# Layer-norm's x1n computed by GpSimd in place of VectorE in a fused two-layer attention kernel

## The chip, the core and the metric

The kernel runs on one core of a Trainium2 chip. The core has a matrix engine (TensorE, PE in the profile), a vector engine (VectorE, DVE), an activation engine (ScalarE, ACT), a general-purpose engine (GpSimd, POOL) and a queue that issues DMAs (SyncE, SP). Each runs its own instruction stream in order and meets the others only at semaphores. The metric is the time of one execution on the device, in microseconds.

## What is computed

The reference takes x and ctx, each 64 x 128 x 512 in fp32, and applies two layers. The first is an attention over time steps with 1x1 convolutions and a residual; the second a transformer layer, in which x1, the first layer's output, is the residual:

```python
x1 = Wo @ (Ml @ softmax(Mn^T @ Mm)^T) + bo + x          # per item, 128 x 512
q  = layer_norm(x1, ln1_w, ln1_b) @ q_w + q_b           # layer_norm: (x1 - mean) * rsqrt(var + eps) * w + b
k, v = ctx @ k_w + k_b, ctx @ v_w + v_b
h  = softmax(q k^T / sqrt(32)) v @ cproj_w + cproj_b + x1     # 16 heads of 32
out = h + gelu(layer_norm(h) @ fc_w + fc_b) @ proj_w + proj_b
```

The part that matters here is x1n = (x1 - mean) * rstd: one mean and one rstd for each of the 128 rows. The weight and bias of the norm are folded into the projection of q.

## The kernel before

The kernel has two passes. The first, `attention_pass`, takes the 64 items one after another in a software pipeline of slots: slot s works on the first layer of item s (b0), on the end of the first layer of item s-1 (b1), on v, q and k of item s-2 (b2), on the scores and softmax of item s-4 (b4), and on the output of item s-5 (b5). The first seven slots and the last are written out; the ones between are a loop whose body has four slots. Keys are projected for two items at once in slots of even parity, queries in slots of odd parity. The second pass, `mlp_pass`, is untouched by the change.

All matmuls are made in three passes on an upper and a lower half of each operand: ScalarE copies the upper half (`_hi`, rounded), and VectorE or GpSimd subtracts it from the original to get the lower half (`_lo`). The order of the work on each engine is the order of the statements in the function `slot` of that engine.

The path of x1 through a slot boundary: at the end of a slot VectorE adds bias and residual into x1 (L884), takes its statistics (L887, L897, L899), and adds x1b of an older item into hid (L905), which goes out to memory. GpSimd makes rstd by a power (L582), then x1b, the sum of x1 and the projection's bias cproj_bias (L588, a ring of four in the tile that the profile calls stage; it waits for hid of four items before), then ctxT_lo, the lower half of the transposed context (L591), and after it multiplies the four quarters of the probabilities by the reciprocals of their sums (L560). In the next slot TensorE makes the scores (L1006, L1011), projects v (L919 to L921 on bank 2), transposes x1n (L950, four instructions, for which it waits for x1n_set) and then multiplies normed by the convolutions' weights; in a slot of queries the projection of q follows, which waits for xnT_lo. VectorE meanwhile takes maxima of the scores (L783), between the second and third of which stands the normalisation x1n (L804, in place: x1n is x1), then a reciprocal (L779), v plus its bias (L813) and xnT_lo (L759). ScalarE takes xnT_hi from the transposes (L655), then m_hi (L659), exponentials (L633), the bias of q or k (L642, L648) and at_hi (L674), whose lower half at_lo is again VectorE's (L759, then the maxima of L789).

Of the kernel before, what the change touches and what calls it, by code (L numbers as in the profile page):

```python
# [18 lines left out]
ALU = mybir.AluOpType  # L19
# [168 lines left out]
def attention_pass(nc, x, ctx, mask, w, hidden, mlp):  # L188
# [8 lines left out]
    with ExitStack() as stack:  # L197
        def sb(name, shape, dt=F32):
            return stack.enter_context(nc.sbuf_tensor(name, shape, dt))

        def sem(name):
            return stack.enter_context(nc.semaphore(name))
# [38 lines left out]
        x1 = sb("x1", [P, D])  # L241
        x1b = stage[:, 0, :, :]
        x1n = x1
# [24 lines left out]
        x1_mv = sb("x1_mv", [P, 2])  # L268
        x1_ve = sb("x1_ve", [P, 1])
        x1_rstd = sb("x1_rstd", [P, 1])  # L270
# [62 lines left out]
        x1_veps = sem("x1_veps")  # L333
        x1_rstd_ready = sem("x1_rstd_ready")
        x1n_set = sem("x1n_set")
        x1b_set = sem("x1b_set")
        xnT_turned = sem("xnT_turned")
        xnT_hi_set = sem("xnT_hi_set")
# [28 lines left out]
        def weight_hi(i, c):  # L367
            return mlp.first_hi[:, i, c, :] if i < 2 else qc_hi[:, i - 2, c, :]

        def weight_lo(i, c):  # L370
            return mlp.first_lo[:, i, c, :] if i < 2 else qc_lo[:, i - 2, c, :]
# [20 lines left out]
        def slots(eng, slot, ahead=None):  # L392

            for s in range(FIRST, LOOPED):
                if ahead and s in ahead:
                    ahead[s]()
                slot(Batch(0, s, B))
            with eng.Fori(0, TURNS) as turn:
                for s in range(LOOPED, LOOPED + Batch.period):
                    slot(Batch(turn, s, B))  # L400
            for s in range(LOOPED + Batch.period * TURNS, LAST + 1):
                if ahead and s in ahead:
                    ahead[s]()
                slot(Batch(0, s, B))
# [4 lines left out]
        def pair_half(t, e):  # L409

            return t[:, :, e.parity, :]
# [126 lines left out]
        @block.gpsimd  # L538
        def _(pool):
            pool.memset(ident[:], 0.0).then_inc(ident_zero, 1)  # L540
            pool.wait_ge(ident_zero, 1)
            pool.affine_select(out=ident[:], in_=ident[:], compare_op=ALU.not_equal, fill=1.0, base=0,
                               pattern=[[-1, P]], channel_multiplier=1).then_inc(ident_set, 1)
            pool.wait_ge(consts_set, 3)

            def lower_halves(i):

                pool.wait_ge(raw_w_in[i], RAW_W_IN[i])
                for c in range(DC):
                    pool.wait_ge(w_hi_set, 4 * i + c + 1)  # L550
                    pool.tensor_tensor(weight_lo(i, c), raw_w[i][:, c, :], weight_hi(i, c).bitcast(F32),
                                       ALU.subtract).then_inc(w_lo_set[i], 1)

            def slot(s):
                b0, b1, b2, b3, b4, ahead = s, s + -1, s + -2, s + -3, s + -4, s + 1

                def normalise(r):
                    if b4.exists():
                        pool.wait_ge(rsum1_set, b4.nth(4, r + 1))
                        pool.tensor_tensor(probs[:, :, r, :, :], probs[:, :, r, :, :],  # L560
                                           rsum1[:, r, :].unsqueeze(1).unsqueeze(3).to_broadcast([P, 4, 4, 32]),
                                           ALU.mult).then_inc(probs_set, 1)

                if b0.first():
                    lower_halves(K_W)
                for r in range(4):
                    normalise(r)
                if ahead.exists():
                    pool.wait_ge(in_veps, ahead.nth(1, 1))
                    if ahead.has_before(1):  # L570
                        pool.wait_ge(normed_set, (ahead + -1).nth(2, 2))
                    pool.tensor_tensor(in_rstd[:], in_ve[:], neghalf[:, 0:2], ALU.pow).then_inc(in_rstd_ready, 1)
                if ahead.exists():
                    for i in range(2):
                        pool.wait_ge(normed_hi_set, ahead.nth(2, i + 1))
                        pool.tensor_tensor(normed_lo[:, i, :], normed[:, i, :],  # L576
                                           normed_hi[:, i, :].bitcast(F32), ALU.subtract).then_inc(normed_lo_set, 1)
                if b1.exists():
                    pool.wait_ge(x1_veps, b1.nth(1, 1))
                    if b1.has_before(1):  # L580
                        pool.wait_ge(x1n_set, (b1 + -1).nth(1, 1))
                    pool.tensor_tensor(x1_rstd[:], x1_ve[:], neghalf[:, 0:1], ALU.pow).then_inc(x1_rstd_ready, 1)  # L582
                    pool.wait_ge(x1_set, b1.nth(1, 1))
                    if b1.has_before(4):
                        pool.wait_ge(hid_set, (b1 + -4).nth(1, 1))
                    else:
                        pool.wait_ge(vecs_in, 16 * 6)
                    pool.tensor_tensor(x1b[:, b1.quarter, :], x1[:], cproj_bias[:], ALU.add).then_inc(x1b_set, 1)  # L588
                if b0.exists():
                    pool.wait_ge(ctxT_hi_set, b0.nth(1, 1))  # L590
                    pool.tensor_tensor(pair_half(ctxT_lo, b0), ctx_chunks, pair_half(ctxT_hi, b0).bitcast(F32),  # L591
                                       ALU.subtract).then_inc(ctxT_lo_set, 1)
                if b3.first():
                    lower_halves(C_W)

            def first_group():

                mlp.inverse_deviations(pool, Item(0, 0, 1))
                for c in range(STAGE):
                    mlp.lower_half(pool, mlp.first_lo[:, 1, c, :], mlp.first_hi[:, 1, c, :], 1, c, mlp_raw[1])  # L600

            slots(pool, slot, {1: lambda: lower_halves(V_W), LAST: first_group})

        @block.scalar
# [112 lines left out]
        def _(dve):  # L717
# [47 lines left out]
            def slot(s):  # L765
                b0, b1, b2, b3, b4, b5, ahead = s, s + -1, s + -2, s + -3, s + -4, s + -5, s + 1
# [14 lines left out]
                def maxima1(r):  # L781
                    if b4.exists():
                        dve.tensor_reduce(negmax1[:, r, :], by_chunk(S1_BANK[r]), AX_X, ALU.max,  # L783
                                          negate=True).then_inc(max1_set, 1)
# [13 lines left out]
                    dve.wait_ge(s1_done, b4.nth(1, 1))  # L798
                maxima1(0)
                maxima1(1)  # L800
                if b2.exists():
                    dve.wait_ge(x1_rstd_ready, b2.nth(1, 1))
                    dve.wait_ge(x1b_set, b2.nth(1, 1))
                    dve.tensor_scalar(x1n[:], x1[:], x1_mv[:, 0:1], x1_rstd[:, 0:1],  # L804
                                      ALU.subtract, ALU.mult).then_inc(x1n_set, 1)
                maxima1(2)
                maxima1(3)
                sum1_reciprocal(0)
# [98 lines left out]
            def statistics():  # L907
                for t in range(TILES):
                    mlp.statistics(dve, Item(0, 0, 1), t)
                for c in range(STAGE):  # L910
                    mlp.lower_half(dve, mlp.first_lo[:, 0, c, :], mlp.first_hi[:, 0, c, :], 0, c, mlp_raw[0])

            slots(dve, slot, {0: prepare_small, 2: prepare_q, LAST - 2: statistics})

        @block.tensor
# [504 lines left out]
```

## Time and profile before

| | |
|---|---|
| median of 3 runs | 3044.06 us (3041.51 to 3044.44) |
| profiled execution | 3044.57 us, its span 3042.8 us |
| PE busy | 2958.4 us, 97% |
| DVE busy | 1873.4 us, 62% |
| ACT busy | 1471.0 us, 48% |
| POOL busy | 790.0 us, 26% |

The span is the time from the first to the last instruction of the profiled execution; its own time has some 2 us around it. Busy shares are over both passes: the attention pass fills about the first 1630 us, and there VectorE, ScalarE and GpSimd are far busier than the averages say. Instructions that only move semaphores, registers or DMAs are not counted.

### The profile page before, as it was taken

To read this page: it belongs to the slowest core of one execution; us is meant where nothing else is said; L and a number is where in the kernel's file an instruction comes from. 1 tells how busy PE (TensorE), PEld (TensorE's weight loads), DVE (VectorE), ACT (ScalarE), POOL (GpSimd) and SP (SyncE) were. 2 spreads that over 40 slices of the span, in tenths; PEclk is the share of its full clock that TensorE was granted. 3 is DMA by queue.
4 is the path that set the end of the run, shared out by engine and by line. 5 is a ranking of instruction groups with operands and counts; after the bars stand their busy time and mean duration, and the time that the engine had idled before them with its cause. 6 is when DMAs were issued, how large, how long until landed. Compare 5 with 4: busy or idle time off the path is not lost. (4 is left out here: it accounts for less than half of the span.)

```text
span 3042.8 us, 55219 instructions
## 1 busy us (share of the span) xinstructions
PE 2958.4 (97%) x18551; PEld 2474.7 (81%) x18551; DVE 1873.4 (62%) x3705; ACT 1471.0 (48%) x4210; POOL 790.0 (26%) x742
## 2 busy tenths in 40 slices
PE   6999999999999999999977999999999999999999
PEld 5788888888888888888865888888888888888887
DVE  6788888888888888888865433333333333333332
ACT  5777777777777777777753211111111111111111
POOL 4444444444444444444422000000000000000000
PEclk9999999999999999999997999999999999999999
DMA  4355555455555445555444211111111111011110
GB/s 125 101 143 141 145 146 143 134 139 142 140 146 146 139 134 141 141 144 147 137 139 138 70 28 28 38 31 41 41 41 41 28 28 37 32 41 41 41 28 14
DMA packets 336371, 281.80 MB, mean 93 GB/s; under 512 B 149056, under 2 KB 247872, under 8 KB 336320
## 3 DMA queue, kind: packets, MB, share of 16 engines
q1 hardware_dynamic: 336320, 281.15, 33.5%
q8 instruction: 28, 0.46, 0.1%
q14 instruction: 23, 0.19, 0.0%
HBM read 164.68 MB, written 100.66 MB: 87 GB/s over the span
## 5 line engine op out<-in xcount | busy, mean ns | idle before, releaser
L1265 ACT ACTIVATE gl<-pre,fc_bias 128x512 f32<-128x512 f32 x256 | 176.6, 690 | 1119.1 <-PE pre L1350 1119.1
L1304 DVE CAST hT_hi<-gl 128x512 fp32r<-128x512 f32 x256 | 109.2, 427 | 838.3 <-ACT gl L1265 838.3
L633 ACT ACTIVATE rows<-bank,negmax 128x128 f32<-128x128 f32 x1024 | 364.1, 391 | 201.4 <-DVE negmax L783 201.4
L560 POOL TENSOR_TENSOR rows<-rows,rsum 128x512 f32<-128x512 f32 x256 | 266.3, 1041 | 370.7 <-DVE rsum L779 370.7
L1348 PE MATMUL pre<-yT_lo,rest_hi 128*128 128x512 f32 x768 | 298.8, 389 | 0.0
L1349 PE MATMUL pre<-yT_hi,rest_lo 128*128 128x512 f32 x768 | 298.8, 389 | 0.0
L1350 PE MATMUL pre<-yT_hi,rest_hi 128*128 128x512 f32 x768 | 298.8, 389 | 0.0
L1348 PE MATMUL acc<-rest_lo,hT_hi 128*128 128x512 f32 x768 | 298.8, 389 | 0.0
L1349 PE MATMUL acc<-rest_hi,hT_lo 128*128 128x512 f32 x768 | 298.8, 389 | 0.0
L1350 PE MATMUL acc<-rest_hi,hT_hi 128*128 128x512 f32 x768 | 298.8, 389 | 0.0
L576 POOL TENSOR_TENSOR normed_lo<-x_ctx,normed_hi 128x512 fp32r<-128x512 f32 x128 | 163.4, 1297 | 333.1 <-ACT normed_hi L699 333.1
L177 POOL TENSOR_TENSOR rstd<-ve,neghalf 128x4 f32<-128x4 f32 x16 | 16.3, 1018 | 870.1 <-DVE ve L171 870.1
L633 ACT ACTIVATION_READ_ACCUMULATOR rows<-bank,negmax 128x1 f32 x1024 | 235.6, 230 | 0.0
L679 ACT ACTIVATE rows<-bank,negmax 128x512 f32<-128x512 f32 x256 | 175.2, 687 | 65.9 <-DVE negmax L789 65.9
L783 DVE TENSOR_REDUCE negmax<-bank 128x4 f32<-128x512 f32 x256 | 164.0, 682 | 35.0 <-PE bank L1011 34.9
L1306 DVE TENSOR_TENSOR hT_lo<-gl,hT_hi 128x512 fp32r<-128x512 f32 x256 | 177.3, 692 | 8.8
L759 DVE TENSOR_TENSOR at_lo<-bank,at_hi 128x512 fp32r<-128x512 f32 x256 | 169.6, 684 | 11.1 <-ACT at_hi L674 6.0
L789 DVE TENSOR_REDUCE negmax<-bank 128x1 f32<-128x512 f32 x256 | 169.4, 682 | 2.9 <-PE bank L921 2.9
L1350 PEld LDWEIGHTS acc<-rest_hi,hT_hi 128*128 128x128 f32 x768 | 144.2, 188 | 30.1
L1349 PEld LDWEIGHTS pre<-yT_hi,rest_lo 128*128 128x128 f32 x768 | 144.3, 188 | 30.0
L1348 PEld LDWEIGHTS acc<-rest_lo,hT_hi 128*128 128x128 f32 x768 | 144.2, 188 | 29.9
L1348 PEld LDWEIGHTS pre<-yT_lo,rest_hi 128*128 128x128 f32 x768 | 144.1, 188 | 29.9
(160 smaller groups left out, 7857.0 us busy)
## 6 DMA issues: line engine op xcount, KB each, us to landing
p_turn<-rows SPq DMA_DIRECT2D x128, 512.0 KB, 3.0
p_blocks<-p_turn SPq DMA_DIRECT2D x256, 256.0 KB, 5.1
x_ctx<-in_x SPq DMA_DIRECT2D x64, 256.0 KB, 6.1
x_ctx<-in_ctx SPq DMA_DIRECT2D x64, 256.0 KB, 6.5
blocks<-in_ctx SPq DMA_DIRECT2D x256, 64.0 KB, 4.8
small<-in_x SPq DMA_DIRECT2D x64, 256.0 KB, 2.7
hidden<-hid SPq DMA_DIRECT2D x64, 256.0 KB, 2.0
rows<-hidden SPq DMA_DIRECT2D x16, 1024.0 KB, 5.5
```

Of the source, the lines that this page charges most:

```text
L560: pool.tensor_tensor(probs[:, :, r, :, :], probs[:, :, r, :, :], rsum1[:, r, :].unsqueeze(1).unsqueeze(3).to_broadcast([P, 4, 4, 32]), ALU ...
L576: pool.tensor_tensor(normed_lo[:, i, :], normed[:, i, :], normed_hi[:, i, :].bitcast(F32), ALU.subtract).then_inc(normed_lo_set, 1)
L633: act.activation(probs[:, :, r, c, :], by_chunk(S1_BANK[r])[:, c, :].rearrange("p (d b) -> p d b", b=32), ACT.Exp, bias=negmax1[:, r, c:c ...
L679: act.activation(A_cols[:, t, :, :, :], bank[S0_BANK[t]][:].rearrange("p (d c x) -> p d c x", d=4, x=32), ACT.Exp, bias=negmax0[:, t:t + 1 ...
L759: dve.tensor_tensor(out, psum, hi.bitcast(F32), ALU.subtract).then_inc(done, 1)
L783: dve.tensor_reduce(negmax1[:, r, :], by_chunk(S1_BANK[r]), AX_X, ALU.max, negate=True).then_inc(max1_set, 1)
L789: dve.tensor_reduce(negmax0[:, t:t + 1], bank[S0_BANK[t]][:], AX_X, ALU.max, negate=True).then_inc(max0_set, 1)
L1265: act.activation(gl[:, i % 2, :], pre[i % 2][:], ACT.Gelu_apprx_tanh, bias=mlp.fc_bias[:, i:i + 1]).then_inc(gelu_done, 1)
L1306: dve.tensor_tensor(hT_lo[:, i % 2, :], gl[:, i % 2, :], hT_hi[:, i % 2, :].bitcast(F32), ALU.subtract).then_inc(hT_lo_set, 1)
L1348: pe.matmul(out, a_hi, b_lo, start=first, stop=False)
L1349: pe.matmul(out, a_lo, b_hi, start=False, stop=False)
L1350: return pe.matmul(out, a_hi, b_hi, start=False, stop=last)
```

## The change

GpSimd computes x1n behind x1b and ahead of ctxT_lo, in the slot in which x1 is made; VectorE computed it in the slot after. The instruction and its operands are the same. GpSimd waits for its own x1_rstd and x1b first, since x1b reads what x1n overwrites.

```diff
@@ GpSimd
                     pool.tensor_tensor(x1b[:, b1.quarter, :], x1[:], cproj_bias[:], ALU.add).then_inc(x1b_set, 1)
+                    pool.wait_ge(x1_rstd_ready, b1.nth(1, 1))
+                    pool.wait_ge(x1b_set, b1.nth(1, 1))
+                    pool.sem_inc(x1_steps, 1)
+                    pool.tensor_scalar(x1n[:], x1[:], x1_mv[:, 0:1], x1_rstd[:, 0:1],
+                                       ALU.subtract, ALU.mult).then_inc(x1n_set, 1)
@@ VectorE
                 maxima1(1)
-                if b2.exists():
-                    dve.wait_ge(x1_rstd_ready, b2.nth(1, 1))
-                    dve.wait_ge(x1b_set, b2.nth(1, 1))
-                    dve.tensor_scalar(x1n[:], x1[:], x1_mv[:, 0:1], x1_rstd[:, 0:1],
-                                      ALU.subtract, ALU.mult).then_inc(x1n_set, 1)
                 maxima1(2)
```

GpSimd's instructions at the end of the loop's first slot, before the change (stage is the tile that holds x1b, rows the probabilities; in brackets the semaphores waited for):

```order
L582 TENSOR_TENSOR x1_rstd<-x1_ve,neghalf 128x1 [waits x1n_set]
L585 REGISTER_ALU [waits x1_set]
L588 TENSOR_TENSOR stage<-x1,cproj_bias 128x512 [waits hid_set]
L590 REGISTER_ALU
L591 TENSOR_TENSOR ctxT_lo<-small_t,ctxT_hi 128x4x128 [waits ctxT_hi_set]
```

And after it, at the same place:

```order
L583 TENSOR_TENSOR x1_rstd<-x1_ve,neghalf 128x1 [waits x1n_set]
L586 REGISTER_ALU [waits x1_set]
L589 TENSOR_TENSOR stage<-x1,cproj_bias 128x512 [waits hid_set]
L593 TENSOR_SCALAR x1<-x1,x1_mv,x1_rstd 128x512 [waits x1_rstd_ready,x1b_set]
L596 REGISTER_ALU
L597 TENSOR_TENSOR ctxT_lo<-small_t,ctxT_hi 128x4x128 [waits ctxT_hi_set]
```

One instruction has come in between x1b and ctxT_lo, and it waits for x1b's end.

VectorE's instructions at the start of the loop's second slot, before the change (the banks are those of the scores, then of v and of the transposes):

```order
L783 TENSOR_REDUCE negmax1<-bank3 128x4
L804 TENSOR_SCALAR x1<-x1,x1_mv,x1_rstd 128x512 [waits x1b_set,x1_rstd_ready]
L783 TENSOR_REDUCE negmax1<-bank6 128x4
L783 TENSOR_REDUCE negmax1<-bank4 128x4
L778 REGISTER_ALU
L779 RECIPROCAL rsum1<-sum1 128x4 [waits exp1_done]
L813 TENSOR_TENSOR stage<-bank2,v_bias 128x512 [waits v_done]
L759 TENSOR_TENSOR xnT_lo<-bank0,xnT_hi 128x4x128 [waits xnT_hi_set]
```

After the change the same rows stand there without the TENSOR_SCALAR; nothing else has moved.

## Rows read from the trace of the kernel before

**Rows 1.** A stretch's busy us (x): PE, PEld, DVE, ACT, POOL; clock, DMA, GB/s
```profile
1000.00:1500.00 500.00, 495.80 (x4012) 420.05 (x4011) 431.13 (x869) 392.21 (x1232) 216.45 (x207) 1.00 0.51 142
```
**Rows 2.** Who waited for whom: us in total, times, longest us
```profile
PE bank L919 <- DVE xnT_lo L759: 10.6, 31, 1.5
```
**Rows 3.** Timeline, TensorE, four slots' first matmuls (start us, us, engine line op, [idle before])
```profile
1034.64 0.40 PE L1006 MATMUL bank<-mask_less,masked_bf 1*128 1x512 bf16 x4
...
1058.92 0.40 PE L1006 MATMUL bank<-mask_less,masked_bf 1*128 1x512 bf16 x4
...
1082.97 0.40 PE L1006 MATMUL bank<-mask_less,masked_bf 1*128 1x512 bf16 x4
...
1107.07 0.40 PE L1006 MATMUL bank<-mask_less,masked_bf 1*128 1x512 bf16 x4
```
**Rows 4.** Timeline, TensorE, slot of queries from 1034.64
```profile
1041.13 0.36 PE L919 MATMUL bank<-xnT_lo,qc_hi 128*128 128x256 f32 x1 [0.40 <-DVE xnT_lo L759]
```
**Rows 5.** Timeline, VectorE, the same slot
```profile
1037.21 1.32 DVE L804 TENSOR_SCALAR x<-x,x_mv,x_rstd 128x512 f32<-128x512 f32 x1
...
1040.31 0.68 DVE L759 TENSOR_TENSOR xnT_lo<-bank,xnT_hi 128x512 fp32r<-128x512 f32 x1
...
1047.04 0.69 DVE L759 TENSOR_TENSOR at_lo<-bank,at_hi 128x512 fp32r<-128x512 f32 x1 [0.24 <-ACT at_hi L674]
```
**Rows 6.** Timeline, GpSimd, the same slot, then x1b of the next
```profile
1035.70 1.29 POOL L588 TENSOR_TENSOR stage<-x,cproj_bias 128x512 f32<-128x512 f32 x1 [0.88 <-DVE hid L905]
1036.94 1.30 POOL L591 TENSOR_TENSOR ctxT_lo<-small_t,ctxT_hi 128x512 fp32r<-128x512 f32 x1
1039.89 1.04 POOL L560 TENSOR_TENSOR rows<-rows,rsum 128x512 f32<-128x512 f32 x1 [1.65 <-DVE rsum L779]
...
1059.80 1.28 POOL L588 TENSOR_TENSOR stage<-x,cproj_bias 128x512 f32<-128x512 f32 x1 [0.77 <-DVE hid L905]
```
**Rows 7.** Timeline, ScalarE, the slot from 1034.64
```profile
1039.37 0.60 ACT L655 ACTIVATE xnT_hi<-bank 128x512 fp32r<-128x512 f32 x1 [1.14 <-PE bank L950]
...
1044.28 0.84 ACT L648 ACTIVATE qT<-bank,q_bias 128x256 f32<-128x256 f32 x2
```
**Rows 8.** The instructions of line 804: duration ns min/median/max, first and last start
```profile
L804 DVE TENSOR_SCALAR x<-x,x_mv,x_rstd x64: 537/1183/1448, 49.4 to 1566.5; 128x512 f32<-128x512 f32 x64
```
**Rows 9.** A group of instructions on GpSimd: xcount | busy us, mean ns | idle before
```profile
L542 POOL TENSOR_SCALAR_AFFINE_SELECT ident<-ident 128x128 f32<-128x128 f32 x1 | 0.3, 292 | 0.2 <-POOL ident L540 0.2
```
**Rows 10.** Timeline, VectorE and ScalarE, slot of queries from 1082.97
```profile
1085.54 1.12 DVE L804 TENSOR_SCALAR x<-x,x_mv,x_rstd 128x512 f32<-128x512 f32 x1
...
1088.44 0.68 DVE L759 TENSOR_TENSOR xnT_lo<-bank,xnT_hi 128x512 fp32r<-128x512 f32 x1
...
1095.24 0.69 DVE L759 TENSOR_TENSOR at_lo<-bank,at_hi 128x512 fp32r<-128x512 f32 x1
...
1087.70 0.60 ACT L655 ACTIVATE xnT_hi<-bank 128x512 fp32r<-128x512 f32 x1 [1.07 <-PE bank L950]
```
**Rows 11.** Timeline, the loop's entry slot, from its first matmul to the next slot's
```profile
165.78 0.40 PE L1006 MATMUL bank<-mask_less,masked_bf 1*128 1x512 bf16 x4
...
168.50 1.43 DVE L804 TENSOR_SCALAR x<-x,x_mv,x_rstd 128x512 f32<-128x512 f32 x1
...
170.74 0.60 ACT L655 ACTIVATE xnT_hi<-bank 128x512 fp32r<-128x512 f32 x1 [1.36 <-PE bank L950]
...
190.31 0.40 PE L1006 MATMUL bank<-mask_less,masked_bf 1*128 1x512 bf16 x4
```
**Rows 12.** Timeline, slot of keys from 1058.92
```profile
1064.84 0.28 PE L919 MATMUL bank<-ctxT_lo,first_hi 128*128 128x256 f32 x1
...
1071.18 0.69 DVE L759 TENSOR_TENSOR at_lo<-bank,at_hi 128x512 fp32r<-128x512 f32 x1
```
**Rows 13.** Timeline, the slot of the second item's x1n
```profile
71.48 1.29 POOL L588 TENSOR_TENSOR stage<-x,cproj_bias 128x512 f32<-128x512 f32 x1
...
74.34 0.33 PE L950 MATMUL bank<-ident,x 128*128 128x128 f32 x1 [1.14 <-DVE x L804]
```

More of the change, by code:

```diff
@@ L335, in attention_pass @@
         x1n_set = sem("x1n_set")
+        x1_steps = sem("x1_steps")
         x1b_set = sem("x1b_set")
```

## The prediction

> **What bounds the kernel now.** I read the page first, then the engines' busy time in a stretch of the attention pass, then who waited for whom, and at last, slot by slot, the order of time on each engine. In the attention pass TensorE is busy 495.8 us of 500, VectorE 431.1, ScalarE 392.2, GpSimd 216.5 [rows 1]. So a microsecond saved on VectorE is worth nothing unless a matmul waits for it, and a microsecond added to GpSimd costs nothing until a matmul waits for it. The waits say where that is: the first matmul of the queries waited 31 times, 10.6 us in all, for VectorE's xnT_lo [rows 2]. That is two instructions behind the one that moves, and it bounds what the attention pass can plainly gain.
>
> The slots repeat in a pattern of four. I measure everything from a slot's first score matmul (L1006). A slot of keys lasts 1082.97 - 1058.92 = 24.05 us; the slot of queries after it 1107.07 - 1082.97 = 24.10; the other slot of queries, the first after each turn of the loop, 1058.92 - 1034.64 = 24.28 [rows 3]. Call them K, Q and Q'. (The fourth is keys again.)
>
> In Q' the chain reads: GpSimd's x1b ends at 1036.99; ctxT_lo runs to 1038.23; VectorE's x1n starts at 1037.21 and takes 1.32 us, to 1038.53; the transposes follow; ScalarE takes the upper half from 1039.37 to 1039.97; but xnT_lo starts only at 1040.31, since VectorE is late by what it did before; the queries' first matmul starts at 1041.13, and TensorE had been idle 0.40 us for it [rows 4 to 7].
>
> **What x1n costs on VectorE.** Alone it takes 0.54 us, its minimum; its median is 1.18 [rows 8]. It ends 0.28 to 0.30 us behind GpSimd's ctxT_lo in Q' (1038.53 against 1038.23) and in the entry slot too, where it takes 1.43 us. So it sits beside a GpSimd instruction and waits most of its time. The Trainium skill, page "SBUF — State Buffer", section "Who interferes with whom", says that VectorE in a 2-port mode and GpSimd exclude each other by a lock on a shared port pair, and that a tensor_reduce never takes part; by it x1n on GpSimd would meet no holder of that lock, as the maxima are reduces. The trace agrees with the first half (1.18 against 0.54 us).
>
> **The change, part by part.** *Removed*: 64 tensor_scalars from VectorE, one a slot, 1.18 us each, between the second and third maxima. The third and fourth maxima, the reciprocal and the sum with v_bias come earlier. The third maximum has no hurry: ScalarE takes its exponentials after xnT_hi and m_hi. The sum with v_bias now waits for the v projection instead, and xnT_lo for xnT_hi.
>
> *Added*: 64 tensor_scalars on GpSimd behind x1b, with a wait for x1b's end. GpSimd has no such instruction before, so its length is bounded by rows. Below: 0.54 us, VectorE's own undisturbed one. A one-input GpSimd instruction of 128 columns takes 0.29; four times that is 1.17. The multiply whose second operand is a few numbers spread over 512 columns takes 1.04; the two-input sum and difference 1.29 and 1.30 [rows 6, 9]. Above: two operations made in two passes of that, 2.6. I take 1.0, by the multiply, the nearest in reading one full stream. For the wait between x1b's end and the start there is one row: GpSimd waited 0.2 us for its own memset before the affine_select [rows 9]. Back to back, ctxT_lo starts 0.05 us before x1b's end. I take 0.15; bounds 0 and 0.25. So x1n ends 1.15 us behind x1b; bounds 0.55 and 2.85.
>
> The Trainium skill, page "GPSIMD Engine Reference", section 4.1, speaks against the move: elementwise work belongs on VectorE, GpSimd is about twice slower with two inputs, and near line rate with one. Twice the 0.54 us would be an estimate of 1.08 us, and the sum below would be the same by it; no run here shows the instruction yet.
>
> *When it is late.* The transposes are behind the v projection on TensorE. In Q' x1n ended at +3.89 and the upper half began at +4.73 (1039.37); in Q it ended at +3.69 (1085.54 + 1.12) and the upper half began at +4.73 as well (1087.70) [rows 5, 7, 10]. So +3.89 still costs nothing. In the loop's entry slot x1n ended at 169.93, +4.15, and the upper half began at 170.74, +4.96, 0.23 late [rows 11]. Beyond about +3.9 each 0.1 us costs 0.1 us. The new end is +2.35 + 1.15 = +3.50 in Q' and 1061.08 - 1058.92 + 1.15 = +3.31 in K and Q [rows 6]: 0.4 to 0.6 us of cover. x1b cannot start earlier, since it waits for hid.
>
> *Moved*: ctxT_lo starts behind x1n, and ends at 2.16 + 1.15 + 1.25 = +4.56 in K. The first matmul of the keys that reads it starts at 1064.84, +5.92 [rows 12]: 1.36 us of cover. Behind it on GpSimd stands the multiply of the first quarter of probs, at 1039.89, +5.25, in Q'; ctxT_lo ends there at +4.75, and the multiply stays where it is. No DMA is issued or passed by, and x1n's readers are the transposes alone.
>
> *What comes back.* With VectorE free, xnT_lo starts when xnT_hi is done, at +5.33, plus 0.03: at +5.36, where it started at 1040.31, +5.67, in Q' and 1088.44, +5.47, in Q. The queries start 0.31 and 0.11 us earlier. But not all of that reaches the slot's end. ScalarE's queue from xnT_hi on (m_hi, two groups of exponentials, the bias, a third group, at_hi) is full: the first at_lo, which waits for at_hi, starts at 1071.18 in K and 1095.24 in Q, both +12.26 to +12.27, though Q's queries start late, and at 1047.04, +12.40, in Q' [rows 5, 10, 12]. In Q' ScalarE has a hole before the bias of the queries (1044.28), and only that closes. So K's 24.05 is the floor: Q' gains 24.28 - 24.05 = 0.23, Q 0.05.
>
> The sum: Q' comes 13 times behind the entry, 13 x 0.23 = 3.0. The loop turns 14 times, so Q comes 14 times, 14 x 0.05 = 0.7. The entry slot lasts 190.31 - 165.78 = 24.53 [rows 11]; its x1n would end at 168.39 (x1b's end, by the 1.25 that ctxT_lo runs beyond it and the 0.28 behind that) + 1.15 = 169.54, in time, so it falls to 24.05: 0.5. The two slots of queries outside the loop, one like Q' and one of 24.17: 0.3. For the second item the transposes waited 1.14 us for x1n, until 74.34; by the 1.15 it ends at 72.77 + 1.15 = 73.92, and they start some 0.1 later [rows 13]: 0.35. The keys' slots, the last slot and the second pass: nothing. Together 4.85, say 4.9 us. The profiled execution took 3044.57 us for a span of 3042.8; less 4.9 that is 3039.7, and the median of the three runs lies 0.5 below it, so I say 3039.5.
>
> With the bound of 0.55 that early slot gains 0.6 more and nothing else moves: 3039. With 1.6 to 1.7 the entry and early slots give less and the sum is about 3.5: 3041.
>
> **Rivals.**
> - *The tensor_scalar is slow on GpSimd* (two passes, or a slow reading of the two scalars). The place is the transposes of x1n, every slot; it decides from about 1.55 us behind x1b in Q' and 1.7 in the others. Q' still has its 0.23 to give, so the sum crosses zero near 1.8. At 2.25 x1n ends at +4.4 in K and Q and +4.6 in Q': 45 x 0.5 + 15 x 0.45, some 29 us, 3073. At the upper bound of 2.85 it is 0.6 x 60 more: 3109. For it: no row has two operations in one GpSimd instruction, and the 0.29 us for 128 columns already comes to 1.17 for 512 [rows 9]. Against it: subtract and multiply are both among its operations here, each 1.0 to 1.3 us with more to read [rows 6].
> - *ScalarE's queue does not bind* and the whole 0.31 and 0.11 us come through: 15 x 0.31 + 14 x 0.11 + 0.5 + 0.5 = 7.2, 3036.9. For it: ScalarE waits for VectorE's maxima elsewhere. Against it: the equal +12.26 and +12.27.
> - *Nothing comes back*: VectorE's hid or GpSimd's later ctxT_lo shifts x1b within the slot, or xnT_lo still starts late behind the sum with v_bias. 3044. For it: TensorE is busy 99% of the stretch, and the whole wait is 10.6 us.
>
> **The numbers.** Forecast 0.58 (3037.5 to 3042.5 its own range), slow tensor_scalar 0.22, ScalarE not binding 0.10, nothing 0.10. About 0.2%, 6.1 us, is what a measurement can tell from no change. The forecast with 4.9 us lies inside it, with a tenth of its chance beyond: faster 0.10 + 0.06 = 0.16; slower 0.20, since a little of the slow case stays within; same 0.64. The range is 3036 to 3058: the low end holds the case in which ScalarE doesn't bind, the high end a tensor_scalar of up to some 1.85 us, and what is left out is most of the slow case.
>
> **What would show it.** The new rows on GpSimd: tensor_scalar near 1.0 us, from 0.1 to 0.15 us behind x1b. xnT_hi still at +4.73 in every slot; if it is later, the slow rival holds, by just that. xnT_lo at +5.36 in all slots; first at_lo at +12.26 in Q', not at +12.1; slots all near 24.05. ctxT_lo still 1.29. The wait of the queries for xnT_lo, 10.6 us, falls to about 5 but not to nothing. It is wrong if the new instruction takes over 1.5 us, or if slots shrink below 24.0.

## The result, and the profile after

| | before | changed |
|---|---|---|
| median of 5 runs on one chip | 3044.44 us (3041.51 to 3045.85) | 3075.45 us (3072.91 to 3075.78) |
| span of the profiled execution | 3042.8 us | 3071.8 us |
| DVE, POOL busy | 1873.4, 790.0 us | 1819.1, 921.2 us |

The ratio is 1.0102, 95% interval 1.0091 to 1.0113: the change costs 31 us. The prediction said 3039.5 us, range 3036 to 3058, and gave 0.22 to the rival that came true, a slow tensor_scalar on GpSimd, for which it had worked out 3073.

The source line of the new instruction first, from the trace of the changed kernel: durations in ns (minimum, median, maximum) and starts, then, behind the lines left out, who waited for it: us in all, times.

```profile
L593 POOL TENSOR_SCALAR x<-x,x_mv,x_rstd x64: 2077/2079/2081, 49.4 to 1594.5; 128x512 f32<-128x512 f32 x64
...
  PE bank L951: 25.4, 63
  PEld bank L951: 4.4, 3
```

It takes 2.08 us where 1.0 was assumed, always, and TensorE waits for it in 63 of 64 slots, where before it waited for xnT_lo in 31 [rows 2]. The timeline of GpSimd in the slot that answers to [rows 6] (start us, us, operation, and idle time before it):

```profile
1053.57 1.29 POOL L589 TENSOR_TENSOR stage<-x,cproj_bias 128x512 f32<-128x512 f32 x1 [0.79 <-DVE hid L906]
1055.06 2.08 POOL L593 TENSOR_SCALAR x<-x,x_mv,x_rstd 128x512 f32<-128x512 f32 x1 [0.20 <-issue]
1057.11 1.28 POOL L597 TENSOR_TENSOR ctxT_lo<-small_t,ctxT_hi 128x512 fp32r<-128x512 f32 x1
1058.35 1.04 POOL L561 TENSOR_TENSOR rows<-rows,rsum 128x512 f32<-128x512 f32 x1
```

x1b ends at 1054.86, x1n 2.28 us later, at 1057.14. On TensorE (the last matmul of v, the transposes, and the first matmul of the queries), against [rows 4]:

```profile
1056.47 0.39 PE L922 MATMUL bank<-first_hi,ctxT_hi 128*128 128x512 f32 x1
1057.29 0.63 PE L951 MATMUL bank<-ident,x 128*128 128x128 f32 x4 [0.42 <-POOL x L593]
...
1059.42 0.36 PE L920 MATMUL bank<-xnT_lo,qc_hi 128*128 128x256 f32 x1
```

Then ScalarE's xnT_hi and VectorE's xnT_lo and first at_lo, against [rows 7] and [rows 5]:

```profile
1057.95 0.60 ACT L661 ACTIVATE xnT_hi<-bank 128x512 fp32r<-128x512 f32 x1 [1.75 <-PE bank L951]
```
```profile
1058.58 0.69 DVE L765 TENSOR_TENSOR xnT_lo<-bank,xnT_hi 128x512 fp32r<-128x512 f32 x1 [0.99 <-ACT xnT_hi L661]
...
1065.46 0.69 DVE L765 TENSOR_TENSOR at_lo<-bank,at_hi 128x512 fp32r<-128x512 f32 x1
```

The reader is to see two things. xnT_lo no longer trails VectorE's backlog: it starts 0.03 us behind xnT_hi, as forecast, and VectorE stands idle 0.99 us before it. But xnT_hi itself is late. The starts of the four slots, against [rows 3]:

```profile
1052.61 0.40 PE L1007 MATMUL bank<-mask_less,masked_bf 1*128 1x512 bf16 x4
...
1077.25 0.40 PE L1007 MATMUL bank<-mask_less,masked_bf 1*128 1x512 bf16 x4
...
1101.79 0.40 PE L1007 MATMUL bank<-mask_less,masked_bf 1*128 1x512 bf16 x4
...
1126.34 0.40 PE L1007 MATMUL bank<-mask_less,masked_bf 1*128 1x512 bf16 x4
```

| us | Q' | K | Q |
|---|---|---|---|
| slot before | 24.28 | 24.05 | 24.10 |
| slot changed | 24.64 | 24.54 | 24.55 |
| xnT_hi starts, before | +4.73 | +4.73 | +4.73 |
| xnT_hi starts, changed | +5.34 | +5.25 | +5.25 |
| difference of the slot | +0.36 | +0.49 | +0.45 |

In K the slot grows by what xnT_hi is late, 0.52, less 0.03. In Q' it grows by 0.25 less than xnT_hi is late, in Q by 0.07 less: that is what the freed VectorE gives back, and the prediction had put it at 0.23 and 0.05. Over the 60 slots from the second one with scores to the last full one (117.44 to 1563.97 us before, 118.04 to 1592.03 changed) this makes 27.5 of the 29.0 us of span. ctxT_lo, which now ends at +5.69 in K, is no second cause: TensorE waits for it once, 0.6 us.

Of the rest the last full slot of the attention pass holds a part: 18.14 us, 16.07 before. Of its 2.07 us, 0.58 are the late xnT_hi; the other 1.49 are lost between the first matmul of q and the product with v behind it (4.53 us, 3.04 before), where many matmuls followed one another every 0.21 us in place of every 0.12. (The slot behind it took 0.60 less than before.) Stretches of 4 us of each kernel, from the same point of that slot: us, then busy us (and count) of PE, PEld, DVE, ACT, POOL, the granted clock, and DMA. Changed, and then before:

```profile
1600.00:1604.00 4.00, 4.00 (x44) 3.87 (x47) 1.39 (x4) 1.28 (x7) 1.70 (x2) 0.71 0.94 306
```
```profile
1572.00:1576.00 4.00, 4.00 (x58) 3.67 (x57) 0.93 (x4) 2.79 (x13) 1.23 (x3) 1.00 0.88 295
```

The granted clock is 0.71 against 1.00: part of the stretch at the lower of the two levels, 1.2 GHz, behind a stretch in which TensorE had been busy only 2.1 of 4 us. Before the change it had been busy 2.5 of 4 us at the same place, and the clock stayed at 1.00.

### The profile page after: what moved, and what is told of

It reads as the page before. It is cut to its first block and busy times, and to the rows that moved or that the text cites. A ratio compares the mean times of both kernels' runs of the same rounds, so it can differ in the third digit from the quotient of the medians.

```text
span 3071.8 us, 55219 instructions
## 1 busy us (share of the span) xinstructions
PE 2966.8 (97%) x18551; PEld 2468.6 (80%) x18551; DVE 1819.1 (59%) x3641; ACT 1463.1 (48%) x4210; POOL 921.2 (30%) x806
## 5 line engine op out<-in xcount | busy, mean ns | idle before, releaser
L1226 POOL TENSOR_TENSOR rows<-rows,proj_bias 128x512 f32<-128x512 f32 x64 | 83.0, 1298 | 325.5 <-DVE y L183 320.4
L1350 PEld LDWEIGHTS acc<-rest_hi,hT_lo 128*128 128x128 f32 x768 | 144.2, 188 | 30.0
L1351 PEld LDWEIGHTS pre<-yT_hi,rest_hi 128*128 128x128 f32 x768 | 144.2, 188 | 30.0
```

The source lines that it names most:

```text
L1350: pe.matmul(out, a_lo, b_hi, start=False, stop=False)
L1351: return pe.matmul(out, a_hi, b_hi, start=False, stop=last)
```

## The experiments

What stood open: whether the price of x1n on GpSimd is all of it, what that price consists of, and whether the return that the prediction promised exists at all. Each ratio is to runs of the kernel before that were made beside the variants; their median was 3043.37 us for the first four, 3044.15 for the next three and 3043.98 for the last. Places such as +4.73 are us from a slot's first score matmul, in the profiled execution.

### Half and three quarters of the columns

```diff
-                    pool.tensor_scalar(x1n[:], x1[:], ...
+                    pool.tensor_scalar(x1n[:, 0:256], x1[:, 0:256], ...      # e1; 0:384 in e2
```

> The changed kernel, but GpSimd normalises only columns 0 to 255 of x1; the others are left as they are (left out: half of x1n). Theory (the tensor_scalar costs by the column, 2.08 us for 512, and the transposes wait for it): the new row takes about 1.1 us, x1n ends about 1.3 us behind x1b, the upper half of xnT starts at +4.73 again, slots last 24.05 to 24.1, and the kernel comes out where the prediction put it, 4 to 5 us below the one before: about 3039.5. Rival (a fixed cost, the fetch of the two scalars, makes most of the 2.08): the row stays above 1.8 us and the time near 3068 or more. Rival (VectorE's freed time gives nothing back): row 1.1 us, but the time equals the one before, 3044.

> The changed kernel with columns 0 to 383 normalised by GpSimd (left out: a quarter of x1n). Theory: row about 1.6 us, x1n ends about 1.8 us behind x1b, +4.0 in slots of keys and in Q, +4.05 in Q'; that is 0.05 to 0.15 us beyond the cover of +3.9, against 0.05 and 0.23 us given back in Q and Q': the crossing point, 3042 to 3047. If the cost is mostly fixed: 3070 and more.

The groups of the new instruction (xcount | busy us, mean ns of one | idle before it), e1 and then e2:

```profile
L593 POOL TENSOR_SCALAR x<-x,x_mv,x_rstd 128x256 f32<-128x256 f32 x64 | 78.5, 1226 | 12.9 <-issue 12.1 <-POOL stage L589 0.8
```
```profile
L593 POOL TENSOR_SCALAR x<-x,x_mv,x_rstd 128x384 f32<-128x384 f32 x64 | 106.0, 1656 | 12.9 <-issue 12.1 <-POOL stage L589 0.8
```

With 2.079 us for 512 these lie on a line: 3.3 ns a column and 0.37 us fixed. Half: 3036.9 us against 3043.37, ratio 0.9981 (0.9972 to 0.9990), which is 6.5 us faster, 2.6 below the forecast. x1n ends 1.43 us behind x1b, xnT_hi starts at +4.73 and xnT_lo at +5.36 in every slot, the first at_lo at +12.25, and the slots last 24.03 to 24.09. Three quarters: 3047.51 us, ratio 1.0015 (1.0006 to 1.0025), 0.5 above the forecast's upper end; x1n ends at +4.02 to +4.11, and xnT_hi starts at +4.83 to +4.92. In the profiled execution 1.4 us of that came in one place: the second slot with scores took 25.68 us, 24.28 before, with a granted clock of 0.57 over 117 to 121 us. So the time follows the end of x1n against +3.9, and the crossing lies where the prediction had it, "zero near 1.8": at 1.43 us behind x1b a gain, at 1.86 us a loss.

### Nobody normalises

```diff
-                    pool.tensor_scalar(x1n[:], ...        # and its waits
-                    pe.wait_ge(x1n_set, b2.nth(1, 1))
+                    pe.wait_ge(x1b_set, b2.nth(1, 1))
```

> Neither engine normalises x1; the transposes take x1 itself and wait for x1b in place of x1n (left out: x1n). Theory: this is the most that freeing VectorE can give, the same 4 to 6 us as with half the columns, 3038 to 3040.5, slots at 24.05 since ScalarE's queue from xnT_hi on is the floor; the first at_lo stays at +12.26. Rival (ScalarE is no floor): slots of queries fall to 24.0 and below and the time to 3036 to 3037. Rival (nothing comes back): 3044.

3038.13 us, ratio 0.9986 (0.9977 to 0.9995): 5.2 us below the kernel before, as forecast. The first at_lo starts at +12.26, and slots last 24.05 to 24.09. But it is not the most that can be had: half the columns and the next kernel came out 1.2 us lower still. The intervals overlap, and the profiled executions show a reason: the slot before the last full one took 23.56 us here and 21.98 with half the columns, 21.97 in the next kernel. The same stretch here and then in the next kernel (columns as above; 0.57 and 1.00 are the granted clock):

```profile
1548.00:1552.00 4.00, 4.00 (x29) 3.03 (x18) 1.81 (x3) 0.66 (x2) 0.00 (x0) 0.57 0.39 135
```
```profile
1548.00:1552.00 4.00, 4.00 (x29) 3.41 (x22) 1.73 (x4) 1.20 (x2) 0.00 (x0) 1.00 0.40 135
```

So taking x1n from VectorE is worth 5 to 6.5 us by these three kernels.

### x1n ahead of x1b

```diff
-        x1n = x1
+        x1n = x_res                                   # reloaded behind xnT_turned in place of x1_set
                     pool.wait_ge(x1_set, b1.nth(1, 1))
+                    pool.wait_ge(x1_rstd_ready, b1.nth(1, 1))
+                    pool.tensor_scalar(x1n[:], x1[:], ...).then_inc(x1n_set, 1)
                     ...                               # then the wait for hid, and x1b
```

> GpSimd normalises all of x1, 2.08 us, but ahead of x1b and into the residual's tile (whose reload then waits for the transposes of x1n), so it need not wait for hid or x1b. Theory: only the end of x1n against +3.9 counts, not GpSimd's length. x1n starts at about +0.2 and ends at +2.4, then x1b to +3.7 and ctxT_lo to +5.0, before the keys want it at +5.92: no transposes wait, and the time is 4 to 6 us below the kernel before, 3038 to 3040.5. Rival (a long GpSimd instruction beside VectorE slows VectorE or shifts hid): 3044 or more.

```profile
1029.89 0.55 POOL L583 TENSOR_TENSOR x_rstd<-x_ve,neghalf 128x1 f32<-128x1 f32 x1 [2.07 <-DVE x_ve L900]
1030.64 2.08 POOL L587 TENSOR_SCALAR small<-x,x_mv,x_rstd 128x512 f32<-128x512 f32 x1 [0.20 <-issue]
1032.69 1.30 POOL L594 TENSOR_TENSOR stage<-x,cproj_bias 128x512 f32<-128x512 f32 x1
1033.94 1.29 POOL L597 TENSOR_TENSOR ctxT_lo<-small_t,ctxT_hi 128x512 fp32r<-128x512 f32 x1
```

This is GpSimd's timeline in the slot from 1030.26. The same 2.08 us, but x1n ends at 1032.72, +2.46, and x1b and ctxT_lo run behind it with time to spare. 3036.92 us, ratio 0.9980 (0.9971 to 0.9989): 6.45 us faster than before, 1.1 below the forecast, and some 38 faster than the changed kernel. The length of the instruction costs nothing by itself; it costs because the instruction stands behind hid and x1b. This version beats both.

### What the 2.08 us consist of

```diff
-                    pool.tensor_scalar(x1n[:], x1[:], x1_mv[:, 0:1], x1_rstd[:, 0:1], ALU.subtract, ALU.mult)
+                    pool.tensor_scalar(x1n[:], x1[:], x1_mv[:, 0:1], None, ALU.subtract)          # e5
+                    pool.tensor_scalar(x1n[:], x1[:], 0.25, 2.0, ALU.subtract, ALU.mult)          # e6
```

> The changed kernel with the subtraction of the mean alone in GpSimd's instruction, all 512 columns (left out: the multiply by rstd). The rows so far read 1.226, 1.656 and 2.079 us for 256, 384 and 512 columns: 0.38 us fixed and 3.3 ns a column. Theory (each of the two operations costs its own 1.67 ns a column): 0.38 + 512 x 1.67 ns = 1.23 us, x1n ends 1.43 behind x1b, inside the cover, 3036 to 3040. Rival (the form of the instruction, scalars from memory, costs 3.3 ns a column whatever it computes): 2.08 us and 3073.

> The changed kernel with two operations, but constants in place of the mean and rstd of each row (left out: the right mean and rstd). Theory (the number of operations sets the price): 2.08 us again, time near 3073. Rival (fetching a scalar for each partition costs it): 1.2 us or a little more, near 3038.

```profile
L593 POOL TENSOR_SCALAR x<-x,x_mv 128x512 f32<-128x512 f32 x64 | 100.6, 1572 | 12.5 <-issue 11.7 <-POOL stage L589 0.8
```
```profile
L593 POOL TENSOR_SCALAR x<-x 128x512 f32<-128x512 f32 x64 | 123.5, 1929 | 11.8 <-issue 11.1 <-POOL stage L589 0.8
```

The first row is one operation (e5), the second two with constants (e6). Neither story holds by itself. One operation costs 1.57 us, where 1.23 or 2.08 were expected; the second adds 0.51; constants in place of the scalars of each row save 0.15 (1.93 us, where 2.08 or 1.2 were expected). So even one operation with one full input costs more than the sum of two full tensors beside it (1.29). The times follow: 3041.49 us with one operation (1.5 above the forecast; ratio 0.9992, 0.9983 to 1.0001, not told from no change; x1n ends 1.77 us behind x1b), and with constants a single execution at 3064.18, where x1n ends 2.12 us behind x1b.

### x1n on ScalarE

```diff
+                    # GpSimd: x1_shift = mean * rstd, then times -1
+                    act.wait_ge(x1_shift_set, b2.nth(2, 2))
+                    act.activation(x1n[:], x1[:], ACT.Identity, scale=x1_rstd[:, 0:1],
+                                   bias=x1_shift[:, 0:1]).then_inc(x1n_set, 1)
                     exp1(0)
```

> x1n on ScalarE, ahead of its first exponentials, where it stands idle 2.95 us in every slot for the first maximum; GpSimd makes -mean*rstd for it in two instructions of one column, and x1n goes into the residual's tile. Theory: x1n takes about 0.7 us, from about +1.2 to +1.9, before the first exponentials at +2.1; nothing waits, VectorE stays free, and the time is that of x1n ahead of x1b on GpSimd, 3036 to 3038. Rival: ScalarE's queue, which sets the slot's floor, is pushed back by part of the 0.7 us, 3040 to 3060.

This diff is against the kernel before the change. x1n takes 0.81 us on ScalarE and ends before the first exponentials, for whose maximum ScalarE then still stands idle 0.49 us, and xnT_hi starts at +4.72. 3040.37 us against 3044.15, ratio 0.9988 (0.9979 to 0.9997): faster, but 3.8 us where 6 to 8 were expected. The time lies in the rival's range, but the rival's cause isn't seen: the first at_lo starts at +12.22 to +12.24, not later than with x1n on GpSimd. Two places show where the rest went: slots last 24.06 to 24.10, like those without x1n; and the second slot with scores took 25.69 us, 24.28 before, its matmuls of v at the lower clock. The same matmuls here and in the kernel before (columns as above):

```profile
116.00:120.00 4.00, 4.00 (x42) 3.29 (x39) 2.57 (x6) 2.32 (x9) 3.40 (x5) 0.57 0.54 126
```
```profile
117.60:121.60 4.00, 4.00 (x49) 3.33 (x46) 2.96 (x5) 1.51 (x8) 3.04 (x3) 1.00 0.79 198
```

### A shorter queue on ScalarE

```diff
-                        act.activation(m_hi[:, i, :], bank[b][:], ACT.Identity,
+                        n = T if b0.first() else T // 2
+                        act.activation(m_hi[:, i, 0:n], bank[b][:, 0:n], ACT.Identity,
```

> The kernel with x1n first on GpSimd, and ScalarE's two m_hi instructions cut to 256 columns from the second item on (left out: the upper halves of the other columns of m). It asks whether ScalarE's queue behind xnT_hi is what held every slot at 24.05 us. Theory (it is): the queue gets some 0.4 us shorter, the first at_lo starts at about +11.85 in place of +12.25, the transposes of the probabilities no longer wait for the bias of the keys, slots last 23.7 to 23.85 and the kernel takes 3017 to 3027. Rival (TensorE's own work is the floor): at_lo moves, slots stay at 24.0 to 24.05, 3034 to 3038.

3029.64 us, ratio 0.9958 (0.9942 to 0.9975) to the kernel before, some 7 us below x1n ahead of x1b, half of what was expected. Slots of keys fell from 24.05 to 23.84 us, slots of queries only from 24.05 to 24.01. TensorE's weight loads for the transposes of the probabilities and for their product with v, in a slot of keys, with x1n ahead of x1b (slot from 1054.34) and then with the shorter queue (slot from 1048.23):

```profile
1064.73 0.42 PEld L951 LDWEIGHTS bank<-ident,rows 128*128 128x128 f32 x4 [0.35 <-ACT kT L648]
...
1068.07 0.81 PEld L1069 LDWEIGHTS bank<-y,stage 128*32 128x32 f32 x32 [0.35 <-issue]
```
```profile
1057.91 0.92 PEld L952 LDWEIGHTS bank<-ident,rows 128*128 128x128 f32 x7
...
1061.76 0.81 PEld L1070 LDWEIGHTS bank<-y,stage 128*32 128x32 f32 x32 [0.35 <-issue]
```

The wait of 0.35 us for ScalarE's bias of the keys is gone, the product with v starts at +13.53 in place of +13.73, the first at_lo came at +12.05, and all behind it followed: ScalarE's queue was the floor of these slots. In slots of queries at_lo came at +12.12 in place of +12.26, but TensorE waited for no such bias in either kernel, and the product with v stayed at +13.76. There ScalarE's queue was worth 0.04 us at most; that what is left is TensorE's own work is argued, not shown.

## Why the prediction was wrong

- *What bounds the kernel, and where the wait is* (the 31 waits for xnT_lo): right. Without x1n on VectorE xnT_lo starts at the forecast +5.36, and the waits for it fall to one of 1.5 us, where about 5 us were forecast.
- *What x1n costs on VectorE*, 0.54 us alone and the rest a wait beside GpSimd: right. In the last full slot, where no ctxT_lo runs beside it, it took 0.54 us.
- *The length of the new instruction*: this step failed, and it alone decided the result. "I take 1.0, by the multiply, the nearest in reading one full stream" was a choice between ends of 0.54 and 2.6, and the runs put 2.08 in its place. The row trusted was that of another operation. What cost it here was the tensor_scalar form itself, 1.57 us with one operation, and 0.51 for the second. The one-input row of [rows 9], 0.29 us for 128 columns, also misled: four times it is 1.17. The near line rate for one input, which the prediction cites from the Trainium skill, page "GPSIMD Engine Reference", section 4.1, does not hold for this instruction: 2.08 us, against 0.54 undisturbed on VectorE. The estimate of 1.08 us that was made beside it is as far off as the 1.0.
- *The wait behind x1b*: 0.20 us measured, 0.15 taken, 0.25 the upper bound.
- *The cover to +3.9, and 0.1 us for each 0.1 beyond*: right. Three quarters of the columns end at +4.02 to +4.11, and xnT_hi starts 0.10 to 0.19 later than +4.73; all columns end at +4.43 to +4.53, and it starts 0.52 to 0.61 later. "x1b cannot start earlier" was not quite so: in Q' it ended at +2.25, 0.10 earlier than before.
- *What comes back*, 0.23 in Q', 0.05 in Q, 4.9 us in all: right in sign and place, and in the slots also in size: with x1n ahead of x1b the 59 slots from the second with scores took 4.7 us less than before, where the sum has 4.5 for them. The kernel without x1n measures 5.2 in all, half the columns 6.5. Outside those slots the sum was less good: it had 0.35 for the start and nothing for the slot before the last full one; with x1n ahead of x1b these gave 1.23 and 0.66.
- *ScalarE's queue as the floor*: shown for the slots of keys. For the slots of queries it was wrong: with a shorter queue they lost only 0.04 us. That changes nothing in the sum.
- *The price of the slow rival*: 29 us at 2.25 us behind x1b; 2.28 and 31 us were measured. A low-clock stretch at the end of the pass (1.5 us in that slot, partly given back behind it) was not in it.
- *The chances*: 0.22 for a tensor_scalar above 1.55 us was too little. One unmeasured number decided between 4.9 us faster and 30 slower, and its interval reached from far inside the cover to far beyond it.

## What to carry to other kernels

When work moves to an engine that has never run that instruction in the kernel, ask first what length would break the cover, and place it so that even the worst length fits: here the same 2.08 us gains 6.4 us ahead of x1b and loses 31 behind it. An instruction's price on GpSimd is not read off another operation of the same size. And a gap that one engine's backlog causes can be valued well from the trace alone, slot by slot, if the next queue that would hold the work back is found too.

## What the runs showed that was not expected

- A tensor_scalar on GpSimd over 128 x 512 fp32: 2.08 us with two operations and scalars of each row, 1.93 with constants, 1.57 with one operation; 3.3 ns a column with 0.37 us fixed for the first. A two-input sum of the same size takes 1.29 us.
- Its length does not vary (2077 to 2081 ns in 64), though VectorE takes its last maxima, a reciprocal and the sum with v_bias beside it.
- Stretches at the lower clock near the ends of the pass come in one kernel and not in the next, and lengthen a single slot by 1.4 to 1.6 us, as much as the effects that were looked for there. Granted over 4 us: 0.71 in the last full slot of the changed kernel, 0.57 in the second slot with scores with three quarters of the columns and with ScalarE, 0.57 in the slot before the last full one without x1n; 1.00 at each of these places before. What switches them on isn't shown: in the 4 us ahead of it TensorE was busy 2.25 us both with ScalarE, where the clock fell, and before, where it did not.
